# Gathers of the batch two ahead issued before the scatters in a mixture-of-experts kernel, and one batch fewer with clearing

## What is computed

```python
def reference(...):                       # x: (8, 512, 128)
    x = x + attn_a(layernorm(x), W_attn, b_attn, W_proj, b_proj)
    x = x + ffn(layernorm(x), expert_sel, keys, values)
    x = x + attn_b(layernorm(x), WQ, WK, WV)
    x = x + ffn(layernorm(x), expert_sel, keys, values)

def ffn(x, expert_sel, keys, values):     # 64 experts, 4 per token
    sel = sigmoid(xf @ expert_sel.T)
    sel_val, sel_idx = top_k(sel, 4)
    gates = zeros.at[rows, sel_idx].set(sel_val)
    h = einsum('nd,kde->nke', xf, keys)
    return einsum('nke,kev->nv', relu(h) * gates[:, :, None], values)
```

## Time and profile before

| | |
|---|---|
| median of 3 runs | 1298.56 us (1295.13 to 1302.17) |
| profiled execution | 1301.94 us, of which the span is 1300.1 us |
| POOL busy | 838.2 us (64%) |
| PE busy | 872.1 us (67%) |
| DVE busy | 828.8 us (64%) |
| ACT busy | 485.7 us (37%) |
| mean granted TensorE clock | 0.811 of full |

### The profile page before, as it was taken

The page is one execution under the profiler, slowest core; times in us unless marked ns, Lnnn a source line. Parts: engine busy times, 40 slices in busy tenths (PEclk is TensorE's granted clock), DMA queues, the critical chain, the costliest instruction groups (busy, mean ns, idle before and its releaser), DMA issues.

```text
span 1300.1 us, 20505 instructions
## 1 busy us (share of the span) xinstructions
PE 872.1 (67%) x6298; PEld 587.4 (45%) x6298; DVE 828.8 (64%) x2421; ACT 485.7 (37%) x1249; POOL 838.2 (64%) x1039
## 2 busy tenths in 40 slices
PE   1499998888888986889888764543688710688000
PEld 0133333333333322789877643422688610688000
DVE  3377688878988754665467796683787740376222
ACT  1116655556545452446435421211254300354000
POOL 2214334676775657537899457778883499999775
PEclk9999899889889887889889955555799955798555
DMA  4555363331426133558856301111565401696322
GB/s 122 178 182 182 132 215 115 121 102 54 137 72 218 54 88 114 144 156 237 233 152 185 85 32 50 51 52 40 147 182 153 141 35 38 167 257 185 102 69 57
DMA packets 206538, 163.68 MB, mean 126 GB/s; under 512 B 15968, under 2 KB 191072, under 8 KB 206432
## 3 DMA queue, kind: packets, MB, share of 16 engines
q1 hardware_dynamic: 185696, 112.00, 30.1%
q0 software_dynamic: 16384, 33.59, 8.5%
q10 hardware_dynamic: 4352, 16.78, 3.3%
HBM read 78.94 MB, written 83.36 MB: 125 GB/s over the span
## 4 chain that ended last, share of the span: by engine, by line
PE 36%; POOL 28%; DVE 19%; issue 11%; DMA 2%; SPq 2%; ACT 1%; POOLq 0%; ACTq 0%; DVEq 0%
POOL v_aug L1623 14%; POOL sorted_rows L1610 7%; PE ps L591 6%; POOL w_attn L1606 6%; PE ps L688 5%; PE ps L529 5%; PE ps L697 4%; PE ps L570 3%; PE ps L556 3%; PE ps L677 2%; DVE row_max L1084 2%; DVE x_res L1314 2%; PE ps L636 2%; PE ps L643 1%; SPq L430 1%
## 5 line engine op out<-in xcount | busy, mean ns | idle before, releaser
L1610 POOL DMA_INDIRECT sorted_rows<-xn,dest x256 | 252.0, 984 | 135.5 <-DVE dest L1287 79.2
L1623 POOL DMA_INDIRECT v_aug<-result_rows,dest x256 | 247.0, 965 | 63.1 <-issue 56.9
L873 ACT ACTIVATE arena<-ps 128x512 f32<-128x512 f32 x320 | 183.1, 605 | 119.9 <-PE ps L529 118.6
L1299 DVE COPY arena<-ps 128x512 f32<-128x512 f32 x128 | 88.0, 688 | 148.5 <-PE ps L677 148.4
L1643 POOL TENSOR_SCALAR_AFFINE_SELECT arena<-arena 128x512 f32<-128x512 f32 (+1 forms) x128 | 65.5, 534 | 170.2 <-ACT arena L873 169.9
L688 PE MATMUL ps<-arena 128*128 128x128 f32 x1024 | 150.1, 294 | 24.4 <-DVE arena L1299 20.2
L556 PE MATMUL ps<-arena 64*128 64x128 bf16 (+3 forms) x576 | 146.8, 318 | 24.3 <-DMA arena<-k_parts 22.9
L1606 POOL MEMSET w_attn<- 128x640 f32 x250 | 162.6, 651 | 0.1
L1084 DVE TENSOR_REDUCE row_max<-ps 128x1 f32<-128x512 f32 (+1 forms) x192 | 128.6, 683 | 39.4 <-PE ps L570 38.1
L677 PE MATMUL ps<-ident,arena 128*128 128x128 f32 x512 | 84.9, 293 | 100.8 <-DMA arena<-sorted_rows 57.5
L688 PEld LDWEIGHTS ps<-arena 128*128 128x128 f32 x1024 | 136.6, 208 | 30.3 <-DVE arena L1299 26.6
(11 more groups left out here) (192 smaller groups left out, 1272.7 us busy)
## 6 DMA issues: line engine op xcount, KB each, us to landing
arena<-sorted_rows SPq DMA_DIRECT2D x128, 256.0 KB, 3.8
result_rows<-arena SPq DMA_DIRECT2D x128, 256.0 KB
sorted_rows<-arena ACTq DMA_DIRECT2D x16, 1024.0 KB, 4.5
arena<-q_parts SPq DMA_DIRECT2D x16, 512.0 KB, 4.1
arena<-k_parts SPq DMA_DIRECT2D x16, 512.0 KB, 5.2
q_parts<-parts SPq DMA_DIRECT2D x52, 128.0 KB, 2.5
k_parts<-parts SPq DMA_DIRECT2D x50, 128.0 KB, 2.7
sorted_rows<-xn,dest POOLq DMA_INDIRECT x256, 2.2
```

What stands on the lines that cost most here:

```text
L873: nc.scalar.activation(prob[:, grp % 2, pr % 2, PROB_AT[u]:PROB_AT[u] + T], ps[:, v % 3, :], ACT.Exp, scale=SCALE_A).then_inc(exp_done, 1)
L1610: g.indirect_dma_start(sorted_d[b // HALF][:, :], bass.IndirectOffsetOnAxis(dest[:, 16 * b + n:16 * b + n + 1], 0), xn1[:, b % 2, n // TOP ...
L1623: g.indirect_dma_start(yg[:, b % 2, i // TOPK, C * c:C * c + C], None, result_d[layer][b // HALF][:, :], bass.IndirectOffsetOnAxis(dest[:, ...
```

## The change

In each iteration of the second attention POOL issues the gathers of batch b+2 first and the scatters of batch b-2 after them. At the end the clearings between gathers stop one batch earlier: the gathers of batch 3 of layer 1 have none.

```diff
@@ -1702,6 +1702,8 @@
             for b in range(-1, LAST_IT_B + 1):
                 nxt, late = b + 1, b - 2
                 paced = b < 2 or b > 4
+                if nxt + 1 < B:
+                    gather(0, nxt + 1, paced=paced)
                 if 0 <= late < B:
                     pool.wait_ge(dest_seq, 2 * (B + late) + 2)
                     pool.wait_ge(ln3, 13 * late + 13)
@@ -1710,13 +1712,11 @@
                         scatter(late, n)
                         if paced:
                             rest()
-                if nxt + 1 < B:
-                    gather(0, nxt + 1, paced=paced)
                 if b == B:
                     gather(1, 0, 0, 8)
             gather(1, 0, 8, TT * TOPK)
             for b in range(1, B):
-                gather(1, b, paced=b < HALF)
+                gather(1, b, paced=b < HALF - 1)
```

## The result

| | before | after |
|---|---|---|
| median of 12 runs each | 1297.71 us (1294.5 to 1302.17) | 1304.51 us (1294.71 to 1307.4) |
| ratio | 1 | 1.0044, 95% interval 1.0023 to 1.0066 |
| profiled execution (span) | 1301.94 (1300.1) us | 1298.9 (1297.2) us |
| POOL busy | 838.2 us | 830.4 us |

The change costs 0.44%, 5.7 us of 1297.7 (the two medians are 6.8 us apart); forecast was +3.7, with a range of 1294 to 1310 us. The profiled execution of the changed kernel is one of its shorter ones, and that of the kernel before one of its longer ones. So the two traces can't be set against each other by their ends. In both I count from the first scatter of batch 0; ahead of it only the gathers of batch 4 are new.

What follows compares the result with a forecast made beforehand. The prediction took POOL's issue order as the bound, with the end of batch 3's scatters releasing the rest. It summed +7.1 us there and -3.4 us at the end to +3.7, 1302.3 us, range 1294 to 1310.

Steps and rivals of the forecast that it cites:

- The bound and the gate: Second attention: POOL is the bound, and the end of batch 3's scatters lets the rest of the kernel begin.
- Gathers of batch 4 in the idle time: Before batch 0's scatters: these gathers run from 736.2 to 757.2, inside POOL's 26.4 us wait for destinations.
- The pitch, and the loss of 7.1 us: Iterations 2 to 5: from times per 16 instructions, paced gathers of batch 7 delay batch 3's scatters, costing 28.1 - 21.0.
- Behind the gate: After batch 3's scatters: absence of batch 7's gathers costed at nothing, bounds -3 and +2 us.
- The clock: TensorE before part (1, 0): already at its lower level, 0.50, so longer idling would cost nothing more; not used in the total.
- The tail: Batch 3 of layer 1: 16 fewer clearings free 8.0 us, but a late result store leaves only 3.4 us won.
- Rival 1: End of kernel: unpaced gathers delay the last store, nothing is given back; +7 to +9 us, chance 0.22.
- The sum: Whole kernel: +7.1 - 3.4 = +3.7 us, median 1302.3 us, inside the 0.5% (6.5 us) told from no change.
- the gate term: End of batch 3's scatters, iteration 5: comes later because batch 7's paced gathers go first, +7.1 us.
- rival 2: After 916 us: DVE's progress, not POOL's order, decides, so its 19 us lead comes through; 1283 to 1293 us, chance 0.10.
- rival 4: Before batch 0's scatters: batch 4's gathers start late, none fit POOL's idle time; up to 21 us more, chance 0.03.
- rival 3: End of part (1, 1): the last result store is not late, 8.0 us are won; -0.9 us in total, chance 0.10.

Runs made afterwards that it cites:

- short sets: Sets of four follow-up runs in which the unchanged kernel before is fast, median 1299.4 us in the second set; the table's comparison counts as one too.
- long sets: First and third sets of four follow-up runs, in which the unchanged kernel before is slow: medians 1352.0 and 1358.6 us.

## Why the prediction was right, and where it wasn't

- **The bound and the gate.** Right in the short sets, shown by the run with the scatters of batch 3 first. It was luck that the first comparison was a short one: in the long sets POOL waits for DVE's destinations in iterations 2 to 4, and a ratio near the forecast one (1.0040) comes about in another way there. The three waits of DVE for gathers, the most visible ones in this stage, were worth nothing as long as that order stood.
- **Gathers of batch 4 in the idle time.** Right: 22.3 us ahead of the first scatter, and a wait of 0.92 us is left.
- **The pitch, and the loss of 7.1 us.** Right in kind, too small: 9.5. The forecast's own times, 891.1 against 883.8, make 7.3 and not 7.1. From the gathers of 5 to those of 7 there are 859.13 - 774.02 = 85.1 us where I had 83.2, and the paced gathers of 7 took 28.4 and not 28.1. I took pitches from a stretch in which DVE stood idle for a quarter of the time, because it waited for POOL. After the change DVE is busy for 79% of that stretch instead of 68%, and POOL's instructions in it are longer.

The same 64 instructions of POOL, first before (779.8 to 862.6 us), then after (774 to 859 us):

```profile
L1623 POOL DMA_INDIRECT v_aug<-result_rows,dest x32 | 32.2, 1006 | 9.8 <-issue 9.8
L1610 POOL DMA_INDIRECT sorted_rows<-xn,dest x32 | 31.2, 976 | 9.8 <-issue 9.8
```

```profile
L1610 POOL DMA_INDIRECT sorted_rows<-xn,dest x32 | 33.0, 1032 | 9.7 <-issue 9.7
L1623 POOL DMA_INDIRECT v_aug<-result_rows,dest x32 | 32.6, 1019 | 9.7 <-issue 9.7
```

  The scatters grow from 976 to 1032 ns and the gathers from 1006 to 1019. Two more profiles bear this out: 974 and 1007 ns with the old order (clearing alone), 1032 and 1014 with the gathers first (scatters of batch 3 first). That it is DVE's work that lengthens them fits, but no run changed it alone. I had noticed the 0.8 us in 16 and used it against the second part only; it belonged into the first too. The rule of the Trainium skill ("SBUF — State Buffer", "Who interferes with whom"), that some DVE operations lock out POOL, agrees in direction; the trace shows 85.1 - 82.9 = 2.2 us over 64 instructions, and which of DVE's operations it would be is not shown.
- **Behind the gate.** The part from PE's first page to the destinations of batch 6 took 121.5 us instead of 124.0. This need be no effect of the missing gathers: it was 121.8 and 124.4 in two other profiles with the old order. Costed at nothing, and nothing here speaks against that. The clock fits too: from 899 to 919 us it was at 0.50, the lower level, as in the last 10 us ahead of the gate before, and in the 120 us from its first page on PE is busy for 100.8 us after and 101.4 before.
- **The tail.** Right: 3.4 us forecast, 3.7 in the trace, 3.5 (1.0 to 6.1) in the run of this part alone. The wait was forecast as 4.6 us and is 4.61. Rival 1, that the unpaced gathers delay the last store, did not happen in the short sets; in the long ones it happened, and the run of this part alone lost 12.6 us.
- **The sum.** +3.7 forecast, +5.7 measured; what is missing has the size of what the gate term lacked. With the measured 9.5 it is 9.5 - 3.7 = +5.8. But the one trace gives less: from the first scatter of batch 0 to the last gather 534.3 us against 531.6, and 529.5 in the second profile of the kernel before, so +2.7 to +4.8. Ten of the other eleven executions of the changed kernel are 4 to 9 us longer than the profiled one, and none of them has a profile. Whether these few us lie at the gate too is open.
- **The rivals.** That DVE's head start comes through behind the gate (rival 2) is refuted: an idle time of 46.04 us. That nothing fits into POOL's idle time (rival 4) is refuted by the 0.92 us. That the store is not late (rival 3) is refuted by the wait of 4.61 us.

## What to carry to other kernels

An order of issue is worth what it does to the one group that lets the next stage begin. Look for that group first: here the waits that could be seen were DVE's, and the price was in a group on which nobody seemed to wait for long. When work is moved ahead into idle time, follow the queue to its next gate, and let only as much pass in front as fits; here the same order, stopped one iteration earlier, won 21.7 us where the full one lost some 9 (by the quotient of two ratios), both in short sets. A gain of a few us from denser issue should be tried in several sets of runs, as the sign of the clearing's part hung on the set.

## What was not expected of the hardware

- On one chip the kernel before took 1352.0 us in one set of runs and 1299.4 in another, each median of 17 or more runs, with ranges that don't meet (1342 to 1361, 1293 to 1305).
- In the long sets ACT and DVE, and PE once for 18.0 us, have waits of up to 22 us whose releaser the profile does not show (ACT 62 to 104 us in sum in the second half of an execution, in each of the eight profiles), beside indirect DMAs that POOL issues every 1.25 us. In the short sets' profiles there are none at the same pace.
- A clearing of 0.65 us after an indirect DMA lengthens the pitch from 1.25 to 1.76 us, by 0.5 us and not by 0.65, since the gap that POOL leaves before the next DMA goes from 0.30 to 0.16 us.
